# Three rotating PSUM banks for the exponentials, one bank for the product with V, and a new order around the start of the experts

## The chip, the cores and the metric

The kernel runs on one core of a Trainium2 chip. The metric is device time in microseconds (us), from the start to the end of one execution; less is better. The engines named below are TensorE (PE in the rows, its weight loads PEld), VectorE (DVE), ScalarE (ACT), GpSimd (POOL) and SyncE (SP, which issues most DMAs). Each engine runs its own list of instructions in a fixed order and waits on semaphores that the others raise.

## The reference

It is one transformer block in fp32: attention with 16 heads of 16 on 4 sequences of 1024 tokens, then a mixture of 8 experts on all 4096 tokens, 2 experts for each.

```python
# attention, on the normalised x
scores = einsum('bqhd,bkhd->bhqk', Q, K) / sqrt(16)
alpha  = softmax(scores, axis=-1)          # over all keys
alpha  = where(causal, alpha, 0)           # masked only after the softmax
Y      = einsum('bhqk,bkhd->bqhd', alpha, V)
x      = x + layernorm(Y)
# experts, on the normalised x
w, idx = top_k(softmax(x @ router), 2); w = w / sum(w)
for e in range(8):
    out += combine[:, e] * (gelu(x @ w_fc[e]) @ w_proj[e])
x      = x + layernorm(out)
```

The row maximum and the denominator of the softmax run over all 1024 keys, the product with V over the lower triangle only.

## The kernel before, in words

**Prologue** (to about 165 us): Q, K and V of all tokens are computed and the parts of Q and K go through DRAM.

**Attention** works on 16 groups of 4 heads. A group takes 32 *units* (k = 0 to 31 of `body(p, u)`), and the stages of three successive groups overlap: while group p has its scores computed, groups p-1 and p-2 have their exponentials and their product with V. One unit holds:

- the **score pair** (L1261): two 512-column matmuls into banks 0 and 1 or 2 and 3, which DVE reduces to row maxima (`negmax`, L1701) in one instruction of 1024 columns. The pair of unit k waits until the reduction of unit k-2 is done (`s_max`);
- two **chunks** (L1074, or L1067 for the upper corner that only feeds the denominator): one 512-column matmul each, which ACT exponentiates out of PSUM (L921, L916). They take banks 4 and 5 in turn (`ebank`), so a chunk waits for the exponential of the chunk two before it (`s_expB`). In the last group, from its third chunk on, four banks rotate (`LAST_RING`);
- in 12 of the 32 units a **burst** of the product with V (L1104), after four exponentials and, on the diagonal, POOL's mask (L765). Burst b belongs to one half of the queries: halves 1 and 0 accumulate in banks 7 and 6. In the numbering of this text bursts lie in units 13, 16, 18, 21, 24, 26, 29, 0 (half 1) and 2, 5, 8, 10 (half 0);
- in units 1, 9, 17 and 25 the **transposed maxima** (L1274), through banks 6 and 7, copied by ACT (L905);
- after the last burst of a half: DVE copies the bank out (*copy-out*, L1712, `at_poc`, units 1 and 11), PE transposes the copy back into the same bank (*turn*, L1248, `at_turn`, units 3 and 13), DVE normalises from it (*norm*, L1725 and L1730, `at_norm`, units 5 and 15).

In a unit of before, PE runs turn, burst, first chunk, score pair, maxima, second chunk. From p = 6 on, DVE also does the two layer norms of finished groups in units 7 to 26 (`STEADY`).

**Tail**: bodies p = 16 and 17 have no score pair. Units 0 to 47 counted from p = 16 carry the router (`turn_x`, `logits`, `turn_back`, `choose`, `count`, `place`), the table of the first ten expert tiles (`totals_early`, `list_early`, `take_early`), the first gathers, the last layer norms (`four_*`), and the first product of tile 0 (`AT_FIRST`, L1206). The orders come from the tables of `at_*` numbers. In one unit DVE runs its tail steps ahead of copy-out and norm.

**Experts**: 71 tiles of 128 tokens. For each, PE transposes the gathered rows (L1193, `transpose_x`), DVE copies them (`copy_x`, L1653 and L1657), PE runs the first product (L1206) and, after ACT's gelu (L976), the second (L1220); DVE scales (`copy_y`, L1665), POOL scatters. Tiles 0 to 8 are written out by hand, interleaved with the router's last two groups and with the table of the remaining 61 tiles (`list_late`, L1181; `hot`, L1810 and L1815; `indices`).

## Time and profile before

| | |
|---|---|
| median of 3 runs | 1549.6 us (1548.51 to 1550.6) |
| the profiled execution, its own time | 1549.0 us |
| its span, first to last instruction | 1547.1 us |
| PE busy | 1420.5 us, 92% |
| DVE busy | 925.6 us, 60% |
| ACT busy | 805.0 us, 52% |
| POOL busy | 610.7 us, 39% |
| mean granted TensorE clock | 0.979 of 2.4 GHz |

A matmul's duration in the trace is longer than the time it keeps the array: matmuls overlap, so the distance between starts tells what one costs. Busy shares are averages over the stages. The chain of waits follows the work that ended last backwards; its pieces touch one another, and in a run of matmuls their lengths are those distances.

### The profile page before, as it was taken

The page shows a single profiled execution, that of the slowest core. Times are in us where ns is not written, and L with a number is a line of the kernel's source. Part 1 is how long each engine was busy: PE and PEld are TensorE (multiplying, and loading weights), DVE is VectorE, ACT ScalarE, POOL GpSimd, SP SyncE. Part 2 cuts the span into 40 slices and gives each one's busy share as a digit, 9 for nine tenths or more (in the row PEclk, how much of TensorE's full clock was granted, in tenths as well). Part 3 has the DMA queues.
Part 4 walks back from the last instruction along what each step waited for, and adds up shares of the span by engine and source line. Part 5 has one row for each costly group of instructions (what it writes and reads, how often), then busy time and mean ns, then how long its engine had stood idle before and what let it go on. Part 6 is the DMA issues. An engine that isn't in the chain of part 4 may idle for free.

```text
span 1547.1 us, 28642 instructions
## 1 busy us (share of the span) xinstructions
PE 1420.5 (92%) x9774; PEld 822.8 (53%) x9775; DVE 925.6 (60%) x1740; ACT 805.0 (52%) x1717; POOL 610.7 (39%) x729
## 2 busy tenths in 40 slices
PE   6788999999999999999999997989999999999990
PEld 3444233333333233323332333789999999999990
DVE  4587778777888988898888977761111111111115
ACT  5454777777777777777777787221111111111114
POOL 2234434443454445444444442323333333333335
PEclk9999999999999999999999999999999999999995
DMA  3665632112210222022204141656666666666646
GB/s 126 150 159 136 232 42 42 19 24 42 42 31 12 42 42 36 6 42 42 42 1 96 55 137 61 187 136 174 193 174 177 192 173 176 194 173 177 193 113 221
DMA packets 100405, 166.85 MB, mean 108 GB/s; under 512 B 12400, under 2 KB 67568, under 8 KB 100304
## 3 DMA queue, kind: packets, MB, share of 16 engines
q1 hardware_dynamic: 86192, 146.08, 35.2%
q0 software_dynamic: 13632, 18.69, 7.5%
q10 hardware_dynamic: 480, 0.79, 0.3%
q8 instruction: 56, 0.92, 0.3%
q14 instruction: 45, 0.37, 0.1%
HBM read 130.76 MB, written 34.77 MB: 107 GB/s over the span
## 4 chain that ended last, share of the span: by engine, by line
PE 69%; DVE 17%; issue 6%; ACT 5%; POOL 2%; DMA 2%; ACTq 0%; POOLq 0%; DVEq 0%
PE ps L1206 16%; PE ps L1220 16%; PE ps L1104 11%; DVE negmax L1701 10%; PE ps L1074 9%; PE ps L1261 8%; ACT wfc L921 2%; PE ps L1043 2%; PE ps L1067 2%; POOL wfc L833 1%; DVE x L1519 1%; PE ps L1248 1%; PE ps L1193 1%; DVE mv L1508 1%; ACT yx L848 1%
## 5 line engine op out<-in xcount | busy, mean ns | idle before, releaser
L1701 DVE TENSOR_REDUCE negmax<-ps 128x1 f32<-128x1024 f32 x512 | 606.8, 1216 | 133.9 <-PE ps L1261 132.4
L921 ACT ACTIVATE wfc<-ps 128x512 f32<-128x512 f32 x768 | 436.0, 595 | 166.2 <-PE ps L1074 160.4
L976 ACT ACTIVATE wfc<-ps 128x512 f32<-128x512 f32 x142 | 84.8, 597 | 426.3 <-PE ps L1206 399.6
L1206 PE MATMUL ps<-yx,wfc 128*128 128x128 f32 x2272 | 268.1, 276 | 5.3 <-issue 5.3
L1206 PEld LDWEIGHTS ps<-yx,wfc 128*128 128x128 f32 x2272 | 266.2, 193 | 9.5 <-issue 6.3
L1220 PE MATMUL ps<-arena,wfc 128*128 x1136 | 258.7, 381 | 0.3 <-issue 0.3
L765 POOL TENSOR_TENSOR wfc<-wfc,causal 128x512 f32<-128x512 f32 x128 | 162.5, 1270 | 243.2 <-issue 111.3
L821 POOL DMA_INDIRECT expert_out<-wfc,rt x71 | 112.7, 1587 | 299.6 <-DVE wfc L1665 289.2
L1220 PEld LDWEIGHTS ps<-arena,wfc 128*128 128x128 f32 x1136 | 211.4, 191 | 26.9 <-issue 0.8
L1261 PE MATMUL ps<-arena 96*128 96x512 bf16 x704 | 211.6, 382 | 8.6 <-DMA arena<-qk_parts 5.3
L1074 PE MATMUL ps<-arena 120*128 120x512 bf16 x528 | 202.3, 390 | 12.0 <-ACT wfc L921 0.4
L1104 PE MATMUL ps<-wfc 128*16 128x128 f32 (+4 forms) x2304 | 161.2, 381 | 0.5 <-POOL wfc L765 0.5
L1665 DVE TENSOR_SCALAR wfc<-ps,rt 128x256 f32<-128x256 f32 x71 | 34.3, 483 | 205.0 <-PE ps L1220 205.0
L916 ACT ACTIVATE ps<-ps 128x512 f32<-128x512 f32 x256 | 149.5, 584 | 10.6 <-PE ps L1067 1.0
L1074 PEld LDWEIGHTS ps<-arena 120*128 120x128 bf16 x528 | 50.1, 96 | 183.5 <-ACT wfc L921 117.1
L1653 DVE SCALAR_TENSOR_TENSOR rt<-yx,rt 128x1 f32 (+1 forms) x71 | 15.5, 218 | 201.4 <-PE ps L1193 201.4
L1261 PEld LDWEIGHTS ps<-arena 96*128 96x128 bf16 x704 | 67.8, 99 | 62.6 <-issue 12.0
L1104 PEld LDWEIGHTS ps<-wfc 128*17 128x17 f32 (+1 forms) x2304 | 60.7, 97 | 75.6 <-issue 47.0
L1074 PE MATMUL ps<-wfc 120*128 120x512 bf16 x240 | 93.0, 388 | 6.5 <-ACT wfc L921 0.8
L1261 PE MATMUL ps<-wfc 96*128 96x512 bf16 x320 | 95.6, 379 | 0.3
L1104 PE MATMUL ps<-wfc,vone 128*17 128x128 f32 (+3 forms) x1024 | 94.6, 441 | 1.0
L744 POOL TENSOR_TENSOR arena<-mT,dmask 24x1024 bf16<-24x1024 bf16 x44 | 83.3, 1894 | 14.8 <-ACT mT L905 11.8
(208 smaller groups left out, 1259.7 us busy)
## 6 DMA issues: line engine op xcount, KB each, us to landing
wfc<-in_L_ffn_w_fc SPq DMA_DIRECT2D x71, 1024.0 KB
arena<-qk_parts SPq DMA_DIRECT2D x126, 128.0 KB, 5.4
...
```

The lines of the kernel that those rows point to most:

```text
L744: pool.tensor_tensor(qs[(u - back) % NSL][MROW:MROW + MR, hl, :] .rearrange("p (i q) -> p i q", i=QT), mT[MROW:MROW + MR, :].unsqueeze(1). ...
L765: pool.tensor_tensor(md_sb[b % NET], et_sb[b % NET][:, :, q:q + P], causal[:, :].unsqueeze(1).to_broadcast([P, GH, P]), ALU.mult).then_inc ...
L821: pool.indirect_dma_start(out=ys_d, in_=yslot[t % 2], in_offset=None, out_offset=bass.IndirectOffsetOnAxis(ap=tok[:, t:t + 1], axis=0), co ...
L916: nc.scalar.activation(bk(ebank(c, g)), bk(ebank(c, g)), ACT.Exp, accum_out=den_u[:, (u - back) % NSL, hl, i:i + 1]).then_inc(s_expB, 1)
L921: nc.scalar.activation(et_sb[b % NET][:, hl, :], bk(ebank(c, g)), ACT.Exp).then_inc(s_expB, 1)
L976: nc.scalar.activation(hidT[s][:, 4 * hf:4 * hf + 4, :], bk(1 + hf).rearrange("p (c t) -> p c t", c=4), ACT.Gelu).then_inc(s_ge, 1)
L1074: nc.tensor.matmul(bk(ebank(c, g)), ks[v][0:MROW + MR, hl, i * P:(i + 1) * P], qs[v][0:MROW + MR, hl, hf * 512:(hf + 1) * 512], start=True ...
L1104: ins = nc.tensor.matmul(out[32 * hl:32 * hl + rows, q0:q1], lhs, rhs, start=(i == 0 and piece == 0 and n == 0), stop=False, skip_group_ch ...
L1206: ins = nc.tensor.matmul(bk(1 + hf)[:, c * P:(c + 1) * P], w1[s][:, kc * FF + (4 * hf + c) * P:kc * FF + (4 * hf + c + 1) * P], xsT[:, kc, :],
L1220: ins = nc.tensor.matmul(bk(5 + s)[:, 0:D], hidT[s][:, c, :], arena[:, ds(off + c * D, D)], start=(c == 0), stop=(c == FC - 1))
L1261: ins = nc.tensor.matmul(bk(2 * (k % 2) + hf), qs[u][0:SROWS, hl, i * P:(i + 1) * P], ks[u][0:SROWS, hl, hf * 512:(hf + 1) * 512], start=T ...
L1701: nc.vector.tensor_reduce(negmax[:, hl % 2, i:i + 1], ps[:, 2 * (k % 2):2 * (k % 2) + 2, :], AX.XY, ALU.max, negate=True).then_inc(s_max, 1)
```

## The change

Three things move; no arithmetic is added or removed.

1. **The ring.** Banks 4, 5 and 6 rotate over one list, `RING`, that has in PE's order every turn, chunk and (but for group 0) transposed maxima. Entry n waits until entry n-3 has been read: by ACT's exponential if that was a chunk, by ACT's copy if maxima, by DVE's norm if a turn (`ring_free`). Both halves of the product with V use bank 7; the first burst of a half waits for the copy-out of the half before (`s_poc`) and no longer for a norm two bursts back. `LAST_RING` goes.
2. **Order in a unit.** PE runs turn, score pair, burst, first chunk, maxima, second chunk. The norm moves two units earlier, into the unit of its turn.
3. **Ahead of and in the first experts.** New numbers in the tail tables, tile 0 transposed into bank 2, `copy_x(5)` and `copy_x(7)` earlier on DVE, other places for `list_late` on PE, `gather(2)` ahead of a root on POOL.

```diff
-        at_norm = [x + 2 for x in at_turn]
+        at_norm = list(at_turn)
...
-        LAST_RING = (4, 5, 1, 2)
...
-        at_bn_x, at_var_x, at_root_x, at_scale = (4, 42), (5, 44), (5, 44), (7, 46)
+        at_bn_x, at_var_x, at_root_x, at_scale = (4, 44), (5, 45), (5, 45), (7, 46)
...
-        at_place = [x + 11 for x in at_first]
-        AT_TOTALS, AT_LIST, AT_TAKE, AT_INDEX, AT_ROWS, AT_TURN0, AT_COPY0, AT_FIRST = 25, 28, 29, 31, 36, 39, 40, (43, 44)
+        at_place = [x + 11 + 2 * (i == IN_TAIL - 1) for i, x in enumerate(at_first)]
+        AT_TOTALS, AT_LIST, AT_TAKE, AT_INDEX, AT_ROWS, AT_TURN0, AT_COPY0, AT_FIRST = 25, 29, 29, 31, 34, 39, 40, (43, 44)
...
+        def ring_entries():
+
+            out = []
+            for x in range(PRO, (NGR + 2) * U):
+                p, k = divmod(x, U)
+                out += [("turn", p - back, j) for j, back in due(at_turn, k) if live(p, back)]
+                chunks = [("chunk", p - back, c) for c, back in due(at_chunk, k) if live(p, back)]
+                out += chunks[:1]
+                out += [("maxima", p - back, hl) for hl, back in due(at_m, k) if live(p, back)]
+                out += chunks[1:]
+            return out
...
+            def ring_free(kind, g, x):
+                n = SLOT[kind, g, x] - NRING
+                if n < 0:
+                    return
+                last, g, x = RING[n]
+                if last == "chunk":
+                    pe.wait_ge(s_expB, NCH * g + x + 1)
+                elif last == "turn":
+                    pe.wait_ge(s_norm, 2 * g + x + 1)
+                else:
+                    pe.wait_ge(s_mtc, GH * g + x + 1)
...
-                    wait_pos(pe, s_expB, NCH * g + c - 1)
+                ring_free("chunk", g, c)
...
-                    et, out = et_sb[b % NET], bk(6 + hf)
+                    et, out = et_sb[b % NET], bk(7)
...
-                        wait_pos(pe, s_norm, 2 * (g - 1) + (j + 1))
-                        pe.wait_ge(s_mtc, min(GH * g + M_BEFORE_PV[j], NH) if isinstance(g, int) else
-                                   GH * g + M_BEFORE_PV[j])
+                        wait_pos(pe, s_poc, 2 * g + j)
...
-                if isinstance(t, int) and t == 0 and hf == 0:
-                    pe.wait_ge(s_expB, NCH * NGR)
...
             first_product(4, 0)
             transpose_x(5, 1)
             second_product(4, 0)
-            first_half(5, 1, 0)
+            first_product(5, 1)
             list_late(0)
-            first_half(5, 1, 1)
             list_late(1)
-            list_late(2)
             transpose_x(6, 0)
             off = expert(5)
             second_half(5, 1, off, 0)
+            list_late(2)
             list_late(3)
+            second_half(5, 1, off, 1)
             list_late(4)
-            second_half(5, 1, off, 1)
             list_late(5)
+            first_product(6, 0)
+            transpose_x(7, 1)
             list_late(6)
-            first_half(6, 0, 0)
             list_late(7)
-            first_half(6, 0, 1)
-            transpose_x(7, 1)
             first_product(7, 1)
...
             for i in (6, 7):
                 gates(i)
+            copy_x(5, 1)
...
             for q in range(2):
                 hot(q)
-            copy_x(5, 1)
             copy_y(4, 0)
...
-            for q in range(4, NPR // PCE):
+            for q in range(4, 6):
                 hot(q)
             copy_y(5, 1)
+            for q in range(6, NPR // PCE):
+                hot(q)
+            copy_x(7, 1)
...
-            copy_x(7, 1)
             copy_x(8, 0)
```

The first place is PE in a middle group, from the end of unit 1 to the turn of unit 3. Before (L1074 and L1067 are chunks, L1261 score pairs, L1104 the burst, L1248 the turn):

```order
L1074 MATMUL ps<-arena 128x512 [waits s_expB]
L1104 MATMUL ps<-wfc,vone 17x128 [waits s_expB,s_mtc,s_norm]
L1104 MATMUL ps<-wfc,vone 17x128 x3
L1104 MATMUL ps<-wfc 17x384 x4
L1104 MATMUL ps<-wfc 16x128 [waits s_mask]
L1104 MATMUL ps<-wfc 16x128 x3
L1074 MATMUL ps<-arena 128x512 [waits s_expB]
L1261 MATMUL ps<-arena 128x512 [waits s_max]
L1261 MATMUL ps<-arena 128x512
L1067 MATMUL ps<-arena 128x512 [waits s_expB]
L1248 MATMUL ps<-ident,wfc 128x128 [waits s_poc]
L1248 MATMUL ps<-ident,wfc 128x128 x3
```

The change, from the end of unit 1 to the second chunk of unit 2 (L1094 and L1087 are chunks, L1277 score pairs, L1122 the burst):

```order
L1094 MATMUL ps<-arena 128x512 [waits s_expB]
L1277 MATMUL ps<-arena 128x512 [waits s_max]
L1277 MATMUL ps<-arena 128x512
L1122 MATMUL ps<-wfc,vone 17x128 [waits s_expB,s_poc]
L1122 MATMUL ps<-wfc,vone 17x128 x3
L1122 MATMUL ps<-wfc 17x384 x4
L1122 MATMUL ps<-wfc 16x128 [waits s_mask]
L1122 MATMUL ps<-wfc 16x128 x3
L1094 MATMUL ps<-arena 128x512 [waits s_expB]
L1087 MATMUL ps<-arena 128x512 [waits s_mtc]
```

and, right behind it, units 3 and 4 with the turn (L1267):

```order
L1267 MATMUL ps<-ident,wfc 128x128 [waits s_expB,s_poc]
L1267 MATMUL ps<-ident,wfc 128x128 x3
L1277 MATMUL ps<-arena 128x512 [waits s_max]
L1277 MATMUL ps<-arena 128x512
L1094 MATMUL ps<-arena 128x512 [waits s_expB] x2
L1277 MATMUL ps<-arena 128x512 [waits s_max]
L1277 MATMUL ps<-arena 128x512
L1094 MATMUL ps<-arena 128x512 [waits s_norm]
L1087 MATMUL ps<-arena 128x512 [waits s_expB]
```

The score pair stands ahead of the burst, the burst of unit 2 waits for a copy-out, and the first chunk of unit 4 waits for a norm.

The second place is DVE just before the experts (counted units 41 to 44). Before (L1519 and L1500 are a layer norm's add and statistics, L1450 to L1490 `place(5)`, L1712 the last copy-out; twelve rows of `place(5)` lie between the two pieces):

```order
L1519 SCALAR_TENSOR_TENSOR x1<-yx,rstd,x1 128x256 [waits s_rsy]
L1519 SCALAR_TENSOR_TENSOR x1<-yx,rstd,x1 128x256 x3
L1523 TENSOR_TENSOR shift<-mv,rstd 128x4
L1500 BN_STATS stats<-x1 128x6 [waits s_add]
L1500 BN_STATS stats<-x1 128x6 x3
L1450 TENSOR_TENSOR rt<-rt,ps 128x32 [waits s_rank]
```

```order
L1486 TENSOR_SCALAR gsum<-gtmp 128x4 [waits s_ex2]
L1488 RECIPROCAL gate<-gsum 128x4 [waits s_gate]
L1490 SCALAR_TENSOR_TENSOR gate<-gtmp,gate 128x4 [waits s_gate]
L1712 COPY wfc<-ps 128x512 [waits s_T4,s_pv]
L1512 MEMSET pause 128x1 [waits s_bnx]
```

The change (L1535 and L1516 are the add and the statistics, L1728 the copy-out, L1466 the start of `place(5)`):

```order
L1535 SCALAR_TENSOR_TENSOR x1<-yx,rstd,x1 128x256 [waits s_rsy]
L1535 SCALAR_TENSOR_TENSOR x1<-yx,rstd,x1 128x256 x3
L1539 TENSOR_TENSOR shift<-mv,rstd 128x4
L1728 COPY wfc<-ps 128x512 [waits s_T4,s_pv]
L1516 BN_STATS stats<-x1 128x6 [waits s_add]
L1516 BN_STATS stats<-x1 128x6 x3
L1466 TENSOR_TENSOR rt<-rt,ps 128x32 [waits s_rank]
```

The last copy-out stands ahead of the statistics and of `place(5)`.

## Rows read from the trace of the kernel before

**Rows 1.** Busy us (count) of PE, PEld, DVE, ACT, POOL; clock, DMA share, GB/s

```profile
270.00:900.00 630.00, 603.87 (x4315) 199.44 (x4317) 545.98 (x672) 478.32 (x1044) 279.71 (x379) 1.00 0.22 35
```

**Rows 2.** Waits, 270 to 900 us: engine, line, releaser; total us, times, longest

```profile
PEld ps L1074 <- ACT wfc L921: 141.2, 298, 0.9
DVE negmax L1701 <- PE ps L1261: 81.8, 97, 1.4
```

**Rows 3.** Chain of waits in one group: start us, us, what

```profile
345.40 0.44 PE ps L1248 x4
345.84 0.22 PE ps L1074
346.06 0.43 PE ps L1261 x2
...
360.74 0.65 PE ps L1248 x4
...
377.37 1.21 PE ps L1104 x24
...
389.80 1.20 PE ps L1104 x16
```

**Rows 4.** Timeline: start us, us, engine line op, shapes [idle before <-releaser]

```profile
336.27 0.39 PE L1074 MATMUL ps<-arena 120*128 120x512 bf16 x1
...
336.70 1.74 ACT L921 ACTIVATE wfc<-ps 128x512 f32<-128x512 f32 x3 [0.84 <-PE ps L1074]
...
337.13 3.49 DVE L1701 TENSOR_REDUCE negmax<-ps 128x1 f32<-128x1024 f32 x3 [0.95 <-PE ps L1261]
```

**Rows 5.** Timeline of DVE: the last copy-outs of four groups

```profile
309.76 0.68 DVE L1712 COPY wfc<-ps 128x512 f32<-128x512 f32 x1
...
360.00 0.68 DVE L1712 COPY wfc<-ps 128x512 f32<-128x512 f32 x1
...
563.60 0.68 DVE L1712 COPY wfc<-ps 128x512 f32<-128x512 f32 x1
...
614.56 0.67 DVE L1712 COPY wfc<-ps 128x512 f32<-128x512 f32 x1
```

**Rows 6.** Timeline of DVE: a reduction and the norm behind it

```profile
603.88 1.22 DVE L1701 TENSOR_REDUCE negmax<-ps 128x1 f32<-128x1024 f32 x1 [0.91 <-PE ps L1261]
...
605.30 0.42 DVE L1730 TENSOR_TENSOR yx<-ps,rden 128x256 f32<-128x256 f32 x1
```

**Rows 7.** Timeline of DVE just before the experts

```profile
972.41 1.40 DVE L1500 BATCH_NORM_STATS2 stats<-x 128x6 f32<-128x256 f32 x4
...
977.25 0.69 DVE L1712 COPY wfc<-ps 128x512 f32<-128x512 f32 x1
...
979.63 1.38 DVE L1526 TENSOR_SCALAR yx<-x,mv,rstd 128x256 f32<-128x256 f32 x4 [1.19 <-POOL rstd L717]
```

**Rows 8.** Timeline of PE into the experts

```profile
978.00 0.66 PE L1248 MATMUL ps<-ident,wfc 128*128 128x128 f32 x4 [2.46 <-DVE wfc L1712]
...
979.21 5.23 PE L1220 MATMUL ps<-arena,wfc 128*128 x16 [0.34 <-issue]
...
989.83 3.72 PE L1220 MATMUL ps<-arena,wfc 128*128 x16
```

**Rows 9.** Timeline of DVE and PE around the products of tiles 5 to 7

```profile
1016.04 0.16 DVE L1787 SCALAR_TENSOR_TENSOR tots<-tots,ntile 128x8 f32<-128x8 f32 x1
...
1021.37 0.42 DVE L1657 COPY yx<-ps 128x256 f32<-128x256 f32 x1
...
1021.89 3.76 PE L1206 MATMUL ps<-yx,wfc 128*128 128x128 f32 x16 [4.18 <-issue]
...
1040.27 3.81 PE L1206 MATMUL ps<-yx,wfc 128*128 128x128 f32 x32 [1.08 <-issue]
```

**Rows 10.** Busy time in two stretches of rows 8 and 9, columns as above

```profile
979.30:982.00 2.70, 2.70 (x7) 2.16 (x8) 2.30 (x9) 0.00 (x0) 0.30 (x1) 0.50 0.85 213
1020.00:1025.00 5.00, 3.11 (x14) 3.14 (x15) 2.13 (x6) 0.00 (x0) 2.58 (x2) 0.50 0.58 225
```

More of the change, by code:

```diff
@@ L467, in x_bank, with tx_bank @@
             return 0 if i < IN_TAIL or kc == 0 else 4
+        def tx_bank(t):
+            return 2 if isinstance(t, int) and t == 0 else 7
         def at_tail(x, p, k):
@@ L515, in load_side, with ring_bank @@
                    .then_inc(s_ld[u], 16)
+        def ring_entries():
[8 more added lines that the diff above has]
+            return out
+        RING = ring_entries()
+        NRING = 3
+        SLOT = {x: n for n, x in enumerate(RING)}
+        R0 = (2 - SLOT["turn", NGR - 1, 1]) % NRING
+        def ring_bank(kind, g, x):
+            return 4 + (SLOT[kind, g, x] + R0) % NRING
         def turn_bank(hl, g):
-            return 7 if isinstance(g, int) and g == 0 else 6 + HALVES[M_HALF[hl]]
+            return 7 if g == 0 else ring_bank("maxima", g, hl)
+        assert PRO > U + max(at_m) - U and ring_bank("turn", NGR - 1, 1) == 6
         @block.sync
@@ L811, in _ @@
             groups(pool, body)
+            gather(2)
             root_y(NPAIR + 2, TPC)
-            gather(2)
             root_x(NPAIR + 2, TPC)
@@ L910, in body @@
                         g = p - back
+                        bank = bk(ring_bank("chunk", g, c))
                         act.wait_ge(s_ST, NCH * g + c + 1)
@@ L915, in body @@
                                 wait_pos(act, s_dt, g - 2)
-                            nc.scalar.activation(bk(ebank(c, g)), bk(ebank(c, g)), ACT.Exp,
+                            nc.scalar.activation(bank, bank, ACT.Exp,
                                                  accum_out=den_u[:, (u - back) % NSL, hl, i:i + 1]).then_inc(s_expB, 1)
@@ L920, in body @@
                         wait_pos(act, s_pv, NBU * g + b - NET + 1)
-                        nc.scalar.activation(et_sb[b % NET][:, hl, :], bk(ebank(c, g)), ACT.Exp).then_inc(s_expB, 1)
+                        nc.scalar.activation(et_sb[b % NET][:, hl, :], bank, ACT.Exp).then_inc(s_expB, 1)
             root_c(0, 0)
@@ L1073, in chunk @@
                     pe.wait_ge(s_ex, GH * g + hl + 1)
-                nc.tensor.matmul(bk(ebank(c, g)), ks[v][0:MROW + MR, hl, i * P:(i + 1) * P],
+                nc.tensor.matmul(bk(ring_bank("chunk", g, c)), ks[v][0:MROW + MR, hl, i * P:(i + 1) * P],
                                  qs[v][0:MROW + MR, hl, hf * 512:(hf + 1) * 512],
@@ L1187, in transpose_x @@
             def transpose_x(t, s):
[L1188 to L1189 removed]
+                if isinstance(t, int) and t == 1:
+                    pe.wait_ge(s_poc, 2 * NGR)
                 pe.wait_ge(s_xs[s], 16 * (t // 2 + 1) if isinstance(t, int) else t * 8 + 8 * (2 - s))
@@ L1246, in body @@
                         pe.wait_ge(s_poc, 2 * (p - back) + (j + 1))
+                        ring_free("turn", p - back, j)
                         for t in range(HQ):
-                            ins = nc.tensor.transpose(bk(6 + hf)[:, t * P:(t + 1) * P],
+                            ins = nc.tensor.transpose(bk(ring_bank("turn", p - back, j))[:, t * P:(t + 1) * P],
                                                       po_sb[:, (HQ * hf + t) * P:(HQ * hf + t + 1) * P], ident[:, :])
                         ins.then_inc(s_T4, 1)
-                    pieces(p, u, k)
-                    todo = due(at_chunk, k)
-                    chunk(p, u, *todo[0])
                     if live(p, 0):
@@ L1263, in body @@
                         ins.then_inc(s_S, 1)
+                    pieces(p, u, k)
+                    todo = due(at_chunk, k)
+                    chunk(p, u, *todo[0])
                     for hl, back in due(at_m, k):
@@ L1267, in body @@
                         h = GH * (p - back) + hl
-                        if isinstance(p, int) and h == GH:
-                            pe.wait_ge(s_poz, 1)
                         pe.wait_ge(s_sp, 4 * h + 4)
                         turned[0] += 1
-                        past = p - M_AFTER_NORM[hl]
-                        wait_pos(pe, s_norm, 2 * past + (M_HALF[hl] + 1) if not isinstance(p, int) or past >= 0 else 0)
+                        if p - back:
+                            ring_free("maxima", p - back, hl)
                         nc.tensor.matmul(bk(turn_bank(hl, p - back))[MROW:MROW + MR, 0:P],
```

37 lines of the change are left out of this document (11 added, 26 removed).

## The prediction

> **What bounds the kernel now.** I read the slices of the page first: attention takes PE at nine tenths from about 165 to 900 us, the experts take PE whole from about 1060 to 1500, and what lies between is ragged. The change leaves the loop over the expert tiles alone, so an earlier start there passes to the end one for one. Then the busy table of the middle of attention [rows 1]: PE 96%, but with overlapping durations, DVE 87%, ACT 76%, granted clock 1.00. No engine is full, so the limit is a pattern of waits. The list of waits says which [rows 2]: PE's weight load of a chunk waits for an exponential 298 times, 141.2 us, and DVE waits 81.8 us for score pairs. The chain [rows 3] gives prices as distances: turn 0.44, chunk 0.22, score pair 0.43, burst with a diagonal 1.21. One off the diagonal streams 512 instead of 640 columns, 0.97. The timeline [rows 4] gives ACT 1.74 / 3 = 0.58 for each exponential, starting 0.43 after its chunk starts; DVE (3.49 - 1.22) / 2 = 1.14 for each reduction. A release reaches PE in 0.06 (the copy-out of [rows 5] ends at 360.68, the turn starts at 360.74 [rows 3]).
>
> The period of a group is 50.24 us without layer norms and 50.96 with them, from the last copy-outs [rows 5]. PE's own work in a group is 32 units of 0.87 = 27.8, 8 + 4 bursts of 1.30 and 1.07 (0.09 added around each, an estimate) = 14.7, two turns 0.9, four maxima 1.0 (estimate, 0.25 each): 44.4. Some 5.8 are waits. DVE's own work is 32 x 1.14 + 2 x 0.61 + two norms of about 0.7 [rows 6] = 39 without layer norms.
>
> **The ring, walked.** With those prices I walked PE, ACT and DVE from unit to unit: a chunk starts when PE is free and the exponential two (before) or three (after) entries back is over. As a test, from the burst of unit 24 to that of unit 0 the walk of before gives 12.5; the chain has 389.80 - 377.37 = 12.43 [rows 3]. For the change it gives 12.0. So a third bank wins 0.5 in 8 units, not all of the 1.3 lost there: with a burst and a score pair between chunks ACT still starts late, and then three banks fill. The maxima now take an entry, and hold the second chunk 0.3 each time. Over the 27 units from 5 to the next 0 this is -1.5.
>
> **The turns.** (a) Turn of unit 13: its copy-out waits for a reduction plus 0.61, before and after; but DVE gets its score pairs earlier, being ahead of the burst: walk -0.6. (b) New: the burst of unit 2 waits for the copy-out of unit 1. The score pair of unit 1 comes 0.43 + 1.30 + 0.44 after that of unit 0, then reduction 1.14 and copy-out 0.68: PE stands 0.5 (ends 0 and 1.1; part of it would otherwise go to the maxima's entry). (c) New: the first chunk of unit 4 waits for the norm of unit 3. From that unit's score pair 0.60 + 1.14 + 0.70 + 0.06 = 2.5 (the norm runs from 605.02, where the reduction of 603.88 gives way, to 605.72 [rows 6]), of which PE fills 0.43 + 0.44 + 0.43 = 1.3: +1.1 (ends 0.6 and 1.8). (d) The same in unit 14 is mostly covered by the burst of unit 13: +0.3. Units 0 to 5 come to +1.45 against before, (c) included. Group without layer norms: -1.5 - 0.6 + 0.3 + 1.45 = about -0.4. Queued behind (b) and (c) on PE are ACT's chunks and DVE's next score pair; in those units neither is the bound, both catch up.
>
> With layer norms DVE carries some 5.5 us more in units 7 to 26 (44 to 45 against 39), and there the pair ahead of the burst keeps it fed. The walk gives 50.5 against 50.96: -0.5. Some 5 groups at -0.4 and 10 at -0.5: **-7.0 us**. Even a DVE bound in those 20 units and PE in the other 12 would give a group of 47.
>
> By the Trainium skill, "Perfetto Trace Analysis", Matmuls, independent matmul groups should rotate through different PSUM banks, so that the evacuation of one overlaps the next. The product with V stops doing so, the chunks do it more. By the skill's sentence on the product alone the sum would get (b) and (c) without the ring's gain, which is the slower rival below.
>
> **The tail.** Bodies 16 and 17 lose the fourth bank of the last group, and (b) and (c) come once more: **+1.0** (ends 0 and 3). From DVE's statistics and `place(5)` to the copy-out lie 972.41 to 977.25 [rows 7], while PE is done with the first product of tile 0 at 978.00 - 2.46 = 975.54 [rows 8]. With the copy-out first, the turn starts when PE is free. But in unit 35 the norm now stands ahead of `place(4)` and waits for its turn, which puts DVE 1.2 later. Turn about 976.9 instead of 978.0. The second product of tile 0 took 5.23 against 3.72 for tile 1 [rows 8], at a granted clock of 0.50, the 1.2 GHz level [rows 10], after PE had waited 2.46; without that wait I take 3.7. Then `turn_x(6)` needs the scale that stood at 979.63 to 981.0 [rows 7] and now comes near 982.4 behind `place(5)`, which takes 1.2 back: -1.1 - 1.5 + 1.2, rounded with the rest of the walk to **-1.7** (ends -4 and +2). POOL's root for that scale is two steps later and is in it. The gather of tile 0 two units earlier only meets DVE's `choose(5)`, which is the later: 0.
>
> **Copies of tiles 5 and 7.** PE stands 4.18 before the first product of tile 5 and goes on at 1021.89 [rows 9]. The releaser is `copy_x(5)`, which ends at 1021.37 + 0.42 = 1021.79 and stands on DVE behind the table and two `hot`. In the change it follows the gates, at 1016.04: done near 1016.6, before PE is free at 1021.89 - 4.18 = 1017.71. So 4.18 go. With them goes the half clock [rows 10]: 16 matmuls took 3.76, and 32 at full clock 3.81, so 1.85. `copy_x(7)` moves ahead of the index arithmetic, and the 1.08 before 1040.27 go. Behind it `list_late` gets its first two pieces some 0.3 late. Weights of tile 7 are asked for once the first product of tile 5 ends, earlier too. Sum **-6.8** (ends -7.5 and -3, if a wait for weights comes instead).
>
> **Sum.** -7.0 + 1.0 - 1.7 - 6.8 = -14.5. Against the profiled execution's 1549.0 (span 1547.1 and 1.9 around it): 1534.5. The median of the runs is 0.6 higher: **1535 us**. A measurement tells about 0.2%, 3.1 us, from no change.
>
> **Rivals.**
> 1. *Slower: the single bank.* The new waits (b) and (c) come in all 15 groups. If ACT's waits do not shrink (a third bank only shifts them to the maxima's and turn's entries) and (b) and (c) are at their upper ends, a group has +1.1 + 1.8 - 0.6 = +2.3, hence +35 and -8.5 at the experts: 1575. It decides from +0.8 us a group on, where the kernel passes 1552. For it: DVE waits for PE in [rows 2], so a late copy-out finds no slack. Against: the walk agrees with [rows 3]. Chance 0.09.
> 2. *The ring does all it could.* PE's waits for exponentials vanish, some 3 us a group more than in my walk: 1549 - 14.5 - 45 = about 1490. Against: the units with a burst need 1.73 us between chunks and ACT has 3 x 0.58 = 1.74 in hand only if all three banks are full. Half of it, 1512, is as near. Chance 0.13.
> 3. *Attention unchanged, experts earlier.* The gains and the new waits cancel: 1549 - 8.5 + 1 = 1541.5. Chance 0.13.
> 4. *The early copies do nothing*, because the weights of tile 5 or 6 land late: 1549 - 8 = 1541. Chance 0.04, and if attention is no gain either, 1548, 0.03.
> 5. *The clock falls in attention.* [Rows 1] has 1.00 with waits of at most 0.9 us [rows 2]; (b) and (c) stay near 1. If one stretch of 2 us at the low level came in each group, as at tile 0, 15 x 1.5 = +22 and the sum of the rest -14.5: 1557. Chance 0.03. The Trainium skill, "TensorE: Matmul & The Clock Gate", in "A second HAM failure mode: psum-queue depth-cycling", describes such swings in a kernel that cycles PSUM banks. Two banks cycle in this trace without any.
>
> **Numbers.** My forecast has 0.55, with its own range of 1526 to 1543. Range over all, 1515 to 1548: it takes in rivals 3 and 4 and half of rival 2, and leaves out rivals 1 and 5 and the full rival 2. Faster by over 0.2%: the forecast, 2, 3 and most of 4: 0.83. Within it 0.06, from the edge of 3 and 4. Slower 0.11, from 1 and 5.
>
> **What would show it.** Right: period of a group 49.6 to 50.0 without and about 50.4 with layer norms; waits of chunks for exponentials down by a third; a wait of bursts for the copy-out of about 0.5, and of chunks for norms of about 1, once a group; no PE wait over 1 us between 1000 and 1045; clock 1.00 in attention. Wrong: waits of 1.5 us and more in units 2 to 4, a group of 51 or over, or the 4 us at tile 5 still there with another releaser.

## The result

The changed kernel takes **1553.88 us** (median of 10 runs, 1552.46 to 1555.35), beside 1549.42 us of the kernel before (10 runs, 1547.85 to 1550.94). The ratio is 1.0029, 95% interval 1.0019 to 1.0039: slower by 4.5 us. The profiled execution took 1552.65 us, with a span of 1550.7 at a mean clock of 0.981 (before: 1547.1, 0.979). The forecast was 1535.

### The profile page after: what moved, and what is told of

Read it like the earlier page. It is cut to its first block, busy times and chain, and to the rows that moved or that the text cites. A ratio compares the mean times of both kernels' runs of the same rounds, so it can differ in the third digit from the quotient of the medians.

```text
span 1550.7 us, 28662 instructions
## 1 busy us (share of the span) xinstructions
PE 1393.8 (90%) x9774; PEld 822.1 (53%) x9775; DVE 944.7 (61%) x1740; ACT 771.5 (50%) x1717; POOL 611.5 (39%) x729
## 4 chain that ended last, share of the span: by engine, by line
PE 66%; DVE 21%; issue 5%; ACT 3%; POOL 2%; DMA 2%; ACTq 0%; POOLq 0%; DVEq 0%
PE ps L1222 16%; PE ps L1238 15%; DVE negmax L1717 11%; PE ps L1122 10%; PE ps L1277 9%; PE ps L1094 7%; PE ps L1087 2%; PE ps L1054 2%; DVE x L1535 2%; DVE mv L1524 1%; DVE wfc L1728 1%; POOL wfc L843 1%; ACT ps L927 1%; PE ps L1267 1%; PE ps L1211 1%
## 5 line engine op out<-in xcount | busy, mean ns | idle before, releaser
L932 ACT ACTIVATE wfc<-ps 128x512 f32<-128x512 f32 x768 | 423.0, 598 | 237.1 <-PE ps L1094 233.3
L987 ACT ACTIVATE wfc<-ps 128x512 f32<-128x512 f32 x142 | 84.8, 597 | 423.6 <-PE ps L1222 423.6
L775 POOL TENSOR_TENSOR wfc<-wfc,causal 128x512 f32<-128x512 f32 x128 | 162.1, 1267 | 297.2 <-issue 153.4
L1277 PE MATMUL ps<-arena 96*128 96x512 bf16 x704 | 212.0, 383 | 18.4 <-DVE negmax L1717 10.6
L1094 PE MATMUL ps<-arena 120*128 120x512 bf16 x528 | 185.7, 388 | 24.4 <-DVE yx L1746 13.7
L1122 PE MATMUL ps<-wfc 128*16 128x128 f32 (+4 forms) x2304 | 161.3, 382 | 0.1
L927 ACT ACTIVATE ps<-ps 128x512 f32<-128x512 f32 x256 | 153.8, 601 | 0.0
L1094 PEld LDWEIGHTS ps<-arena 120*128 120x128 bf16 x528 | 47.3, 97 | 153.2 <-ACT wfc L932 49.6
L1277 PEld LDWEIGHTS ps<-arena 96*128 96x128 bf16 x704 | 63.9, 99 | 93.2 <-DVE negmax L1717 26.1
L1122 PEld LDWEIGHTS ps<-wfc 128*17 128x17 f32 (+1 forms) x2304 | 60.4, 98 | 87.5 <-issue 63.1
L1122 PE MATMUL ps<-wfc,vone 128*17 128x128 f32 (+3 forms) x1024 | 95.5, 445 | 7.3 <-DVE wfc L1728 7.3
L1277 PE MATMUL ps<-wfc 96*128 96x512 bf16 x320 | 95.7, 380 | 4.5 <-DVE negmax L1717 4.2
L1094 PE MATMUL ps<-wfc 120*128 120x512 bf16 x240 | 84.0, 384 | 14.0 <-DVE yx L1746 8.7
```

The source lines that it names most:

```text
L775: pool.tensor_tensor(md_sb[b % NET], et_sb[b % NET][:, :, q:q + P], causal[:, :].unsqueeze(1).to_broadcast([P, GH, P]), ALU.mult).then_inc ...
L927: nc.scalar.activation(bank, bank, ACT.Exp, accum_out=den_u[:, (u - back) % NSL, hl, i:i + 1]).then_inc(s_expB, 1)
L932: nc.scalar.activation(et_sb[b % NET][:, hl, :], bank, ACT.Exp).then_inc(s_expB, 1)
L987: nc.scalar.activation(hidT[s][:, 4 * hf:4 * hf + 4, :], bk(1 + hf).rearrange("p (c t) -> p c t", c=4), ACT.Gelu).then_inc(s_ge, 1)
L1094: nc.tensor.matmul(bk(ring_bank("chunk", g, c)), ks[v][0:MROW + MR, hl, i * P:(i + 1) * P], qs[v][0:MROW + MR, hl, hf * 512:(hf + 1) * 512 ...
L1122: ins = nc.tensor.matmul(out[32 * hl:32 * hl + rows, q0:q1], lhs, rhs, start=(i == 0 and piece == 0 and n == 0), stop=False, skip_group_ch ...
```

## The profile after

The busy table of the changed kernel for the middle of attention, to be held against [rows 1]: us in the stretch, then busy us and count of PE, PEld, DVE, ACT and POOL, the granted clock, the DMA share and GB/s.

```profile
270.00:900.00 630.00, 571.36 (x4232) 195.67 (x4230) 555.32 (x664) 441.40 (x1022) 274.20 (x374) 1.00 0.23 35
```

The clock stayed at 1.00. DVE is busy 9.3 us more than before although it executes 8 instructions fewer in the stretch. That is the first sign: some of its instructions take longer, it does not run more of them.

The list of waits of the changed kernel, same stretch, answers to [rows 2]: engine and line, the releaser, total us, times, longest. Lines have moved: the chunk L1074 is L1094, the score pair L1261 is L1277, the exponential L921 is L932, the norm L1730 is L1746, the copy-out L1712 is L1728.

```profile
ACT wfc L932 <- PE ps L1094: 184.7, 188, 2.1
...
DVE negmax L1717 <- PE ps L1277: 72.8, 111, 1.6
...
PEld ps L1094 <- ACT wfc L932: 53.2, 136, 0.9
...
PEld ps L1094 <- DVE yx L1746: 29.1, 24, 1.4
...
PE ps L1094 <- DVE yx L1746: 17.3, 24, 0.9
...
PE ps L1122 <- DVE wfc L1728: 5.4, 12, 0.5
```

The ring did its work: PE's waits of chunks for exponentials fall from 141.2 us [rows 2] to 53.2. ACT waits longer for chunks instead: 184.7 us, against 122.5 in the kernel before. The two new waits are there at the size forecast: the burst stands 5.4 / 12 = 0.45 for the copy-out, and the chunk 17.3 / 24 = 0.7 for the norm.

Where the time went is read from the last copy-out of each group, as in [rows 5]. The timeline of DVE in the changed kernel: start us, us, engine, line and shapes.

```profile
308.02 0.68 DVE L1728 COPY wfc<-ps 128x512 f32<-128x512 f32 x1
...
357.90 0.68 DVE L1728 COPY wfc<-ps 128x512 f32<-128x512 f32 x1
...
408.46 0.67 DVE L1728 COPY wfc<-ps 128x512 f32<-128x512 f32 x1
...
512.96 0.67 DVE L1728 COPY wfc<-ps 128x512 f32<-128x512 f32 x1
...
565.20 0.68 DVE L1728 COPY wfc<-ps 128x512 f32<-128x512 f32 x1
...
912.26 0.69 DVE L1728 COPY wfc<-ps 128x512 f32<-128x512 f32 x1
```

A group without layer norms takes 49.88 us (before: 50.24), a group with them 52.25 (before: 50.97 on the mean). Here is the same account for the whole kernel. Its marks are copy-outs: of before at 209.29, 410.71 and 903.16, of the change at 208.26, 408.46 and 912.26 (the third is the first copy-out of the tail, in unit 1 of p = 16):

| stretch | before | after | difference | forecast |
|---|---|---|---|---|
| three groups without layer norms and one in whose last units they begin | 201.42 | 200.20 | -1.2 | -1.6 |
| 9.7 groups with them | 492.45 | 503.80 | **+11.35** | about -5 |
| from there to the end | 643.94 | 638.44 | -5.5 | -7.5 |

The three add up to +4.6; the medians differ by 4.5. (The first of these marks lies between 206.7 and 211.4 us in the kernels of this study, also in those that differ only behind it, so I count from it on.) One row of the table, the groups with layer norms, holds 16 of the 19 us that the forecast missed.

**What lengthened DVE's instructions.** Mean durations in the list of groups, 400 to 900 us. First the kernel before, then the changed one (line, engine, operation, shapes and count, busy us and mean ns, idle time before).

```profile
L1519 DVE SCALAR_TENSOR_TENSOR x<-yx,rstd,x 128x256 f32<-128x256 f32 x20 | 15.3, 767 | 0.0
...
L1508 DVE TENSOR_SCALAR mv<-mv 128x2 f32<-128x2 f32 x10 | 12.1, 1211 | 0.3
...
L1516 DVE TENSOR_SCALAR mv<-mv 128x2 f32<-128x2 f32 x10 | 1.7, 169 | 0.3
```

```profile
L1535 DVE SCALAR_TENSOR_TENSOR x<-yx,rstd,x 128x256 f32<-128x256 f32 x20 | 24.1, 1206 | 0.0
...
L1524 DVE TENSOR_SCALAR mv<-mv 128x2 f32<-128x2 f32 x10 | 18.6, 1858 | 0.3
...
L1532 DVE TENSOR_SCALAR mv<-mv 128x2 f32<-128x2 f32 x10 | 1.7, 170 | 0.3
```

L1524, the last instruction of `var_y`, works on two numbers per partition and takes 1.86 us. L1532, the same form on the same shape in `var_x`, takes 0.17. The timelines of DVE and POOL show what differs. The changed kernel, `var_y` in unit 9 and the second `add` in unit 17:

```profile
522.12 1.89 POOL L754 TENSOR_TENSOR wfc<-mT,dmask 24x1024 bf16<-24x1024 bf16 x1 [1.33 <-ACT mT L915]
...
561.11 1.89 POOL L754 TENSOR_TENSOR arena<-mT,dmask 24x1024 bf16<-24x1024 bf16 x1
```

```profile
522.36 1.94 DVE L1535 SCALAR_TENSOR_TENSOR x<-yx,rstd,x 128x256 f32<-128x256 f32 x1
...
561.17 1.86 DVE L1524 TENSOR_SCALAR mv<-mv 128x2 f32<-128x2 f32 x1
```

And the kernel before in the same units:

```profile
572.54 1.89 POOL L744 TENSOR_TENSOR arena<-mT,dmask 24x1024 bf16<-24x1024 bf16 x1 [0.73 <-ACT mT L905]
...
610.47 1.89 POOL L744 TENSOR_TENSOR arena<-mT,dmask 24x1024 bf16<-24x1024 bf16 x1
```

```profile
573.65 1.06 DVE L1519 SCALAR_TENSOR_TENSOR x<-yx,rstd,x 128x256 f32<-128x256 f32 x1
...
611.19 1.19 DVE L1508 TENSOR_SCALAR mv<-mv 128x2 f32<-128x2 f32 x1
```

In all four pairs the end of the DVE instruction follows that of the GpSimd product beside it: `var_y` ends with the product and the add 0.3 us behind it (561.17 + 1.86 = 563.03 and 561.11 + 1.89 = 563.00; 611.19 + 1.19 = 612.38 and 610.47 + 1.89 = 612.36). In the kernel before `var_y` came 0.72 us into that product, now 0.06: nearly all of it is waited out. The add came 1.11 into it and now comes 0.24 into it. I call the part over the bare duration "held". Bare are 0.17 for `var_y`, 0.475 for an add, 0.40 for a scale. A group of the kernel before has 1.04 + 2 x 0.29 + 2 x 0.19 = 2.0 us held, one of the changed kernel 1.69 + 2 x 0.73 + 2 x 0.20 = 3.5.

The Trainium skill, "SBUF — State Buffer", Who interferes with whom, says that GpSimd and VectorE share a pair of ports as an exclusive lock: a `tensor_scalar` in a two-port mode, or an instruction with two inputs in SBUF, waits in full for a GpSimd instruction that started first (and, for the second form, reads SBUF), and `tensor_reduce` does not. The rows agree: 1.69 us held for the first form and 1.47 for the second (1.94 - 0.475), while reductions beside the same product, as in e3 below, keep their 1.2 us. Which mode `var_y` runs in, the trace does not show.

**Theory A**: the change moves `var_y` and the second `add` under GpSimd's product, DVE loses some 1.5 us more a group, and as DVE is nearly full there, the group gets longer. **Rival B**: the loss is the ring's own, from chunks behind the norm in units 4 and 14 and from DVE waiting for pairs; the held instructions sit in slack.

## Experiments

### VectorE's steps moved away from GpSimd's product

`e1_after_vary8` and `e2_after_add15` each move one of the steps of the changed kernel (e1 takes the statistics that `var_y` needs, `bn_y`, along), `e3_after_both` both and a scale; `e4_before_both` has the three moves in the kernel before.

```diff
 # e1: var_y earlier
-STEADY = {7: ("bn_y", 0), 8: ("bn_y", 1), 9: ("var_y", 0), 13: ("add", 0), 17: ("add", 1),
+STEADY = {6: ("bn_y", 0), 7: ("bn_y", 1), 8: ("var_y", 0), 13: ("add", 0), 17: ("add", 1),
 # e2: add earlier
-STEADY = {7: ("bn_y", 0), 8: ("bn_y", 1), 9: ("var_y", 0), 13: ("add", 0), 17: ("add", 1),
+STEADY = {7: ("bn_y", 0), 8: ("bn_y", 1), 9: ("var_y", 0), 13: ("add", 0), 15: ("add", 1),
 # e3 (in the changed kernel) and e4 (in the kernel before)
-STEADY = {7: ("bn_y", 0), 8: ("bn_y", 1), 9: ("var_y", 0), 13: ("add", 0), 17: ("add", 1),
-          18: ("bn_x", 0), 19: ("bn_x", 1), 20: ("var_x", 0), 24: ("scale", 0), 26: ("scale", 1)}
+STEADY = {6: ("bn_y", 0), 7: ("bn_y", 1), 8: ("var_y", 0), 13: ("add", 0), 15: ("add", 1),
+          18: ("bn_x", 0), 19: ("bn_x", 1), 20: ("var_x", 0), 24: ("scale", 0), 25: ("scale", 1)}
```

> The changed kernel with bn_y and var_y one unit earlier each (6, 7, 8 in place of 7, 8, 9), so that the 128x2 tensor_scalar of var_y is issued before GpSimd's product for the maxima (L754, 1.89 us, 561.11 in the trace of the change) and not beside it. Theory A (VectorE's tensor_scalar stands still until that GpSimd instruction has ended: 1.86 us at 561.17, against .17 for the same form at 528.63): the mean of L1524 falls from 1.86 to about .2, the group with layer norms from 52.25 to about 50.9, and the kernel to 1538 to 1545. Rival B (the loss of 1.3 a group comes from the ring: the chunk of unit 14 behind the norm, maxima behind PE): L1524 may get shorter, the idle time of DVE takes it up, and the time stays at 1554 within 2.

> The changed kernel with the second add of a group at unit 15 in place of 17, ahead of GpSimd's product of unit 18 (522.12, 1.89 us; the add beside it took 1.94 where the first took .47). Theory A: mean of the adds L1535 falls from 1.21 to about .5, 1.3 to 1.5 us a group less on DVE, and the kernel is at 1541 to 1548. Rival B: stays at 1554 within 2, or gets slower, since the add now stands between the norm of unit 13 and the maxima that PE waits for.

> The changed kernel with both steps moved (6, 7, 8 and 15) and the second scale at unit 25 in place of 26 (.81 beside GpSimd's product of unit 26, .40 without it). Theory A: 1.69 + 1.47 + .40 us a group go from DVE, ten groups, of which the idle time of DVE (5.2 us a group) takes up some: 1524 to 1535, and the group near 49.9 to 50.2. Rival B: within 2 us of 1554, with the group at 52.

> The same three moves in the kernel before. There the blocked times were 1.02 (var_y), .59 (add) and .37 (scale) a group. Theory A: 10 to 20 us less, 1530 to 1540, and the change is then worth what the moved-free comparison gives: e3 under e4 by 3 to 12 us (my walk of the ring gave -.5 a group, and the experts -6.8). Rival B: the kernel before stays at 1549 and e3 above it.

Measured beside 1549.72 us of the kernel before (19 runs):

| kernel | us | ratio, 95% interval | group with layer norms |
|---|---|---|---|
| e1 | 1546.76 | 0.998 (0.9971 to 0.9989) | 51.57 |
| e2 | 1542.98 | 0.9961 (0.9947 to 0.9974) | 51.13 |
| e3 | 1537.55 | 0.9919 (0.9906 to 0.9933) | 50.45 |
| e4 | 1546.20 | 0.998 (0.997 to 0.999) | 50.66 |

Rival B falls: a few steps moved by one or two units in DVE's list, with the ring untouched, take 16 us from the changed kernel. The group without layer norms stays at 49.88 in all three. e2 came where Theory A put it; e1 and e3 came 2 to 3 us short of it, and e4 won 3.5 us, not 10 to 20. The kernel before has little to gain from these moves, so the loss belongs to the change; e3 is 8.7 us under e4, where 3 to 12 was expected. What was still held in e1 and e3 is in their rows. The timelines of POOL and of DVE in e3:

```profile
555.80 1.26 POOL L775 TENSOR_TENSOR wfc<-wfc,causal 128x512 f32<-128x512 f32 x1 [0.27 <-ACT wfc L932]
...
557.14 1.89 POOL L754 TENSOR_TENSOR arena<-mT,dmask 24x1024 bf16<-24x1024 bf16 x1
```

```profile
555.85 0.15 DVE L1522 BATCH_NORM_AGGREGATE mv<-stats 128x2 f32<-128x6 f32 x1
...
556.03 1.06 DVE L1524 TENSOR_SCALAR mv<-mv 128x2 f32<-128x2 f32 x1
...
557.00 3.64 DVE L1717 TENSOR_REDUCE negmax<-ps 128x1 f32<-128x1024 f32 x3
```

`var_y` had moved from one product of GpSimd to another, the mask (L775), and ended with it (557.09 and 557.06). The aggregate beside the same mask was not held, and three reductions under the 1.89-us product took 3.64 together.

### All held time away, and what is left of the change

`f1_after_vary12` puts `var_y` where GpSimd is nearly idle. `f2_before_vary12` has the same edit in the kernel before; there the scales were still held, and `m2_before_free` moves those too.

```diff
 # f1, f2
+STEADY = {7: ("bn_y", 0), 8: ("bn_y", 1), 12: ("var_y", 0), 14: ("add", 0), 15: ("add", 1),
+          18: ("bn_x", 0), 19: ("bn_x", 1), 20: ("var_x", 0), 24: ("scale", 0), 25: ("scale", 1)}
+ROOT_Y, ROOT_X = 13, 21
 # m2 against f2
-          18: ("bn_x", 0), 19: ("bn_x", 1), 20: ("var_x", 0), 24: ("scale", 0), 25: ("scale", 1)}
+          18: ("bn_x", 0), 19: ("bn_x", 1), 20: ("var_x", 0), 23: ("scale", 0), 26: ("scale", 1)}
```

> The changed kernel with var_y at unit 12 (its root at 13), the adds at 14 and 15 and the second scale at 25: no GpSimd instruction over .7 us runs there. In e1 and e3 the moved tensor_scalar still took 1.06 us, and ended with the product with the mask of unit 9 (L775, 555.80, 1.26 us): Theory A says any of GpSimd's products holds it, so here it takes .17, the group comes to 49.9 to 50.2 (e3: 50.45), and the kernel to 1531 to 1535. Against A: L1524 stays near 1 us wherever it is put, because it reads what bn_aggr has just written, and the time stays with e3 (1537.6).

> The kernel before with the same moves as f1 (var_y at unit 12 with its root at 13, adds at 14 and 15, second scale at 25), so that neither kernel has a step of the layer norms beside a product on GpSimd. Theory A: L1508 takes .17 here; the group goes from 50.66 (e4) to about 50.5, the kernel to 1544 to 1546, and f1 stands under it by 11 to 12 us: what the change is worth without the blocking. If the blocked time is what the change loses, its gain is then near my forecast for it (-7.0 in the attention and -6.8 in the experts, with +1.3 between). Against A: f2 is as far under before as f1 is under the change (20 us, at 1529), and the moves help any order alike.

> The kernel before with var_y at unit 12, its root at 13, the adds at 14 and 15 and the scales at 23 and 26, where GpSimd runs no product over .7 us. Held time 0 in a group with layer norms. Theory A with the slopes so far (50.97, 50.66, 50.39 at 2.0, 1.3 and .7 us held): 50.2 to 50.35, and the kernel 1541 to 1543. Then the change is worth nothing (0 within .1) in such a group where nothing is held, and my walk's -.5 was wrong there by as much. If it stays at 50.39 or above (the scales were not on any path): the change is worth -.1 there.

f1: **1533.50 us** (4 runs), ratio 0.9893 (0.9877 to 0.991). f2: 1543.05 (5 runs), 0.9959 (0.9945 to 0.9973). m2: 1543.04 (4 runs), 0.9954 (0.9937 to 0.997). So the moves do not help any order alike: beside the kernel before measured with each, f1 wins 16.3 us and f2 6.4, though the change by itself had lost 4.5. f1 is 9.5 us under f2, a little less than the 11 to 12 expected. The rows of f1 by form, 400 to 900 us, have nothing held:

```profile
L1542 DVE TENSOR_SCALAR yx<-x,mv,rstd 128x256 f32<-128x256 f32 x20 | 8.0, 402 | 0.0
L1524 DVE TENSOR_SCALAR mv<-mv 128x2 f32<-128x2 f32 x10 | 1.7, 169 | 0.3
```

Held time (worked out as above from each kernel's means) against the period of a group with layer norms:

| changed kernel and its variants | held us | period | before and its variants | held us | period |
|---|---|---|---|---|---|
| change | 3.5 | 52.25 | before | 2.0 | 50.97 |
| e1 | 2.8 | 51.57 | e4 | 1.3 | 50.66 |
| e2 | 2.1 | 51.13 | f2 | 0.7 | 50.39 |
| e3 | 0.9 | 50.45 | m2 | 0 | 50.39 |
| f1 | 0 | 50.28 | | | |

From e3 up to the change, the changed kernel pays 0.7 us for each held (52.25 - 50.45 = 1.8 for 2.6 us). The kernel before pays 0.45 for each above 0.7 (50.97 - 50.39 = 0.58 for 1.3 us). The last 0.9 and 0.7 us cost 0.17 and nothing. With nothing held the change is worth 50.28 - 50.39 = -0.1 in such a group, and with about 2 us held in both (e2 and before) it costs 0.2. In m2 the slopes did not go on as Theory A had them; it is the other of its two outcomes, in which the scales were on no path.

### GpSimd made to wait, VectorE left alone

So far it was DVE that moved. `m1_after_root9` moves one number of GpSimd's.

```diff
-ROOT_Y, ROOT_X = 10, 21
+ROOT_Y, ROOT_X = 9, 21
```

> The changed kernel with one number changed: GpSimd's root of var_y at unit 9 in place of 10. It waits for var_y, so the product for the maxima of unit 10 (1.89 us), which is behind it on GpSimd, can only start when var_y has ended; no step of VectorE is moved. Theory A: L1524 falls from 1.86 to .17 to .5 us, the group from 52.25 to 51.0 to 51.2, the kernel to 1540 to 1545; the add of unit 17 stays at 1.94. Against A (var_y takes 1.86 for a reason of its own, or GpSimd's later product holds up the chunks that wait for it): L1524 or the group unchanged, 1553 or more.

Measured: 1546.45 us (10 runs), ratio 0.9976 (0.9966 to 0.9986), 7.4 us under the change; group 51.57. Timelines of DVE and POOL:

```profile
559.32 0.17 DVE L1524 TENSOR_SCALAR mv<-mv 128x2 f32<-128x2 f32 x1
559.40 1.22 DVE L1717 TENSOR_REDUCE negmax<-ps 128x1 f32<-128x1024 f32 x1
561.53 1.22 DVE L1717 TENSOR_REDUCE negmax<-ps 128x1 f32<-128x1024 f32 x1 [0.92 <-PE ps L1277]
```

```profile
559.64 0.69 POOL L722 TENSOR_TENSOR rstd<-mv,mhalf 128x2 f32<-128x2 f32 x1 [0.45 <-DVE mv L1524]
560.41 1.89 POOL L754 TENSOR_TENSOR arena<-mT,dmask 24x1024 bf16<-24x1024 bf16 x1
```

`var_y` is at the same place in DVE's list and takes 0.17. It is GpSimd's product that holds it. The period fell by 0.68, less than the 1.1 to 1.2 expected, though all 1.69 us are gone: the second reduction behind it now waits 0.92 for its score pair, so PE is late next. e1, with 0.9 of `var_y` still held, has the same period of 51.57: the last 0.9 us of that instruction were covered there, and are not why e1 fell short. m1 has 1.9 us held and a period of 51.57, e2 has 2.1 and 51.13, so the slope of the table is no law: which step is held counts too.

### Which part of the change moved VectorE under the product

`h2_before_pair_first` puts the score pair ahead of the burst in the kernel before; `h1_after_pair_last` puts it back behind them in the changed kernel.

```diff
 # h2, in PE's body (h1 is the reverse)
+                    if live(p, 0):
...
+                        ins.then_inc(s_S, 1)
                     pieces(p, u, k)
                     todo = due(at_chunk, k)
                     chunk(p, u, *todo[0])
-                    if live(p, 0):
...
-                        ins.then_inc(s_S, 1)
```

> The kernel before with the score pair ahead of the burst and the chunk in each unit, ring of two banks kept. If the order alone made the gain of the groups and the loss of those with layer norms: period 49.9 and 52.2, so 1558 to 1562 (without the experts' gain). If the ring made them: period near 50.24 and 50.97, 1549 within 3.

> The changed kernel with the score pair behind the burst and the chunk again, all else as changed. If pair first carries the gain of .36 a group without layer norms, the period of 49.88 goes to 50.2 or more and that of 52.25 changes with the place of DVE against GpSimd (51 to 53): 1548 to 1562. If order is indifferent (DVE and PE lie bound by what they wait for, not by who comes first): 1554 within 2.

Both missed what I expected, by far. h2: 1580.25 us (4 runs), ratio 1.0201 (1.0184 to 1.0218), groups 52.0 and 53.19. h1: 1612.07 us (4 runs), ratio 1.0401 (1.0384 to 1.0419), groups 54.2 without layer norms and up to 57.5 with them. Neither half of the change can stand alone. Groups without layer norms, where hardly anything is held: 50.24 before, 52.0 with the pair first, 54.2 with the ring and the early norm, 49.88 with both. In h1 the first chunk of unit 14 waits for the norm of unit 13, which stands behind that unit's reduction on DVE, and the pair of unit 14, DVE's next work, stands behind the chunk. The timeline of PE in h1:

```profile
326.00 0.39 PE L1094 MATMUL ps<-arena 120*128 120x512 bf16 x1 [1.93 <-DVE yx L1746]
```

The change has 0.19 at that place (311.99), because there the pair of unit 14 is issued before the wait. Where the 1.8 us a group go that h2 loses without layer norms, I have not traced: PE, ACT and DVE show waits of the same kinds as in the kernel before, and that stays open.

h2 answers the question, too. The timelines of DVE and POOL:

```profile
575.63 1.86 DVE L1508 TENSOR_SCALAR mv<-mv 128x2 f32<-128x2 f32 x1
```

```profile
575.57 1.89 POOL L744 TENSOR_TENSOR arena<-mT,dmask 24x1024 bf16<-24x1024 bf16 x1
```

Same offset as in the change, 0.06 us, with the old ring and the old norm. The order "score pair first" moves DVE's step 0.66 us forward against the product. A likely reason, read from the code and not tried by itself: the reduction of a unit starts with its pair, which now comes earlier in the unit, while the maxima that start GpSimd's product are still turned at the unit's end. What a held step costs differs, too: with as much held as in the change (3.6 us by the same means), a group with layer norms in h2 is only 53.19 - 52.0 = 1.2 us longer than one without, where the change has 2.4.

### The experts and the tail

`g1_before_experts` has only the experts' part in the kernel before. `k4_f1_old_tail` is f1 with the unit numbers of the tail as before; `k1_f1_add_later` is f1 with one tail step moved.

```diff
 # g1: DVE (PE's order from first_product(5, 1) on as in the change)
                 gates(i)
+            copy_x(5, 1)
...
-            copy_x(5, 1)
             copy_y(4, 0)
...
+            copy_x(7, 1)
             nc.vector.tensor_reduce(tabf[:, 0:NLC], cmp_l[0:1, :, :], AX.X, ALU.add).then_inc(s_hic, 1)
 # k4
-at_bn_x, at_var_x, at_root_x, at_scale = (4, 44), (5, 45), (5, 45), (7, 46)
+at_bn_x, at_var_x, at_root_x, at_scale = (4, 42), (5, 44), (5, 44), (7, 46)
-at_place = [x + 11 + 2 * (i == IN_TAIL - 1) for i, x in enumerate(at_first)]
+at_place = [x + 11 for x in at_first]
-AT_TOTALS, AT_LIST, AT_TAKE, AT_INDEX, AT_ROWS, AT_TURN0, AT_COPY0, AT_FIRST = 25, 29, 29, 31, 34, 39, 40, (43, 44)
+AT_TOTALS, AT_LIST, AT_TAKE, AT_INDEX, AT_ROWS, AT_TURN0, AT_COPY0, AT_FIRST = 25, 28, 29, 31, 36, 39, 40, (43, 44)
 # k1
-at_bn_y, at_var_y, at_root_y, at_add = (0, 38), (1, 39), (1, 39), (3, 41)
+at_bn_y, at_var_y, at_root_y, at_add = (0, 38), (1, 39), (1, 39), (4, 41)
```

> The kernel before with only the experts' part of the change: copies of the rows of tiles 5 and 7 earlier on VectorE, the late list's products later on TensorE. My ledger: -6.8, so 1542.5 to 1544; the waits of 4.18 and 1.08 at L1206 are gone. If the -9.5 that the change won between the turn of tile 0 and tile 8 came from elsewhere (the clock, rows waiting for gathers): 1547 to 1550.

> f1 with the numbers of the units behind the last group as they were before the change (bn_x 42, var_x and root_x 44, place(5) at +11, early list at 28, rows at 36). My prediction gave those numbers +.4 to +1 in all with the start of the tail; g1 and the ledger say +1.3 for all that lies between copy-out and turn. If the numbers are worth something to the new ring: k4 slower than f1 by 1 to 4 us. If they are neutral: 1533.5 within 1.

> f1 with the four adds of the first tail step at unit 4 in place of 3. In f1 they stand ahead of the norm of unit 3 on VectorE, 3.41 us at 895.66 and 1.22 of the shift (1.67 and .16 where GpSimd is idle), and PE waits 2.49 us at 900.89 for that norm. Theory (the norm moved two units earlier now stands behind work that it stood ahead of in time): the wait goes to under .5, the copy-out of unit 11 comes 1.5 to 2.5 us earlier, the kernel 1531 to 1532.5. Rival (the unit 7 to 11 work waits for POOL's root and the scale anyway, 4.35 us of idle at 907.12): same as f1, 1533.5.

g1: 1542.07 us (4 runs), ratio 0.9951 (0.9934 to 0.9967). Its profile from the copy-out at 903.21 to the end takes 637.1 us, before it took 643.9: **-6.8**, the forecast to the tenth (-7.7 by the medians). The timeline of PE in g1 has no wait before the products of tiles 5 and 7, which stood 4.18 and 1.08 in [rows 9]:

```profile
1017.89 3.73 PE L1206 MATMUL ps<-yx,wfc 128*128 128x128 f32 x32
...
1033.33 3.79 PE L1206 MATMUL ps<-yx,wfc 128*128 128x128 f32 x32
```

The change takes 638.4 from its copy-out to the end, so the rest of its tail costs 1.3 against g1. k4: 1536.88 us (4 runs), 0.9916 (0.99 to 0.9933): the new unit numbers are worth 3 us to the new ring (from the first copy-out to the end 1325.8 us, f1 1322.8). k1: 1532.14 us (4 runs), 0.9889 (0.9873 to 0.9906). The wait it aims at is gone. PE in f1, then in k1:

```profile
900.89 0.39 PE L1094 MATMUL ps<-wfc 120*128 120x512 bf16 x1 [2.49 <-DVE yx L1746]
```

```profile
895.93 0.39 PE L1094 MATMUL ps<-wfc 120*128 120x512 bf16 x1 [0.23 <-DVE yx L1746]
```

By the medians k1 and f1 can't be told apart (1.4 us, overlapping intervals, measured beside different runs of the kernel before). In the profiled executions it is 1.9 us from the first copy-out to the end. So k1 is probably the fastest kernel here; that both are 16 to 17 us faster than the kernel before, and some 20 faster than the change, is shown.

## Why the prediction was wrong

- **The walk of the ring, groups without layer norms: right.** Forecast -0.4, measured -0.36 in each. The waits of chunks for exponentials fell by more than the third that was forecast, from 141.2 to 53.2 us, and the group still won no more than that: rival 2 is out. In the group from 308 to 358 us the waits (b), (c) and (d) are 0.45 (341.13), 0.92 (345.76) and 0.19 (311.99), forecast 0.5, 1.1 and 0.3. The clock stayed at 1.00, so rival 5 is out, as is rival 1 in its mechanism: the single bank does not cost more than it was given.
- **The step that failed: "With layer norms DVE carries some 5.5 us more in units 7 to 26 (44 to 45 against 39), and there the pair ahead of the burst keeps it fed. The walk gives 50.5 against 50.96: -0.5."** Measured +1.28 a group. The walk took the 5.5 us as a constant carried over from the kernel before. 2.0 us of them were no work of DVE at all but time held by GpSimd, and that depends on when DVE comes, which is the very thing the change moves. In the change they became 3.5. f1 and m2 size it: with the held time gone the change wins 52.25 - 50.28 = 1.97 a group and the kernel before 50.97 - 50.39 = 0.58; the difference is 1.39 of the 1.78 us between forecast and result. Both kernels also had steps moved to other units for it, so part of the 1.39 may be the place of the steps and not the holding. m1, which leaves DVE's order alone, shows 0.68 of it for `var_y`; the adds and scales were not tried that way. The other 0.39 is the walk itself, which gave -0.5 where -0.1 is left with nothing held. What it overlooked there no run settles. In the stretch this is 16 us of the 19 that the forecast missed.
- **The order of the forecast's gain made the loss.** "The pair ahead of the burst keeps it fed" names the cause of the harm: h2 shows that this order alone brings `var_y` to 0.06 us behind the start of the product.
- **Copies of tiles 5 and 7: right.** -6.8, shown by g1. There the first product of tile 5 takes 3.73 us for 32 matmuls where 16 took 3.76 [rows 9], so the half clock went with the wait, as forecast.
- **Tail start and tile 0: too good by 2.** Forecast +1.0 and -1.7, measured +1.3 in all. From the first copy-out of the tail to the turn ahead of tile 0's second product lie 78.7 us in the change and 74.8 before, and what is behind the turn is 2.4 us shorter than in g1. Of the 3.9, 2.4 lie between the first two copy-outs (16.0 against 13.7): the norm of unit 3 stood behind four adds of 3.41 us and made PE wait 2.5. k1 takes that wait away. In my walk the norm, two units earlier, had only the reduction in front of it on DVE. The other 1.5 I put down to the norm of unit 35, which waits for its turn. I had put DVE 1.2 late for that. The timeline of DVE shows 3.53, and that of PE a wait of 3.64 for DVE's `oh_bf`, which the router's `choose` writes behind it:

```profile
972.18 0.26 DVE L1741 RECIPROCAL rden<-ps 128x16 f32<-128x16 f32 x1 [3.53 <-PE ps L1267]
```

```profile
983.13 0.21 PE L1173 MATMUL ps<-oh_bf,lower 128*128 128x32 bf16 x1 [3.64 <-DVE oh_bf L1455]
...
985.82 5.32 PE L1222 MATMUL ps<-yx,wfc 128*128 128x128 f32 x32
...
991.63 3.62 PE L1238 MATMUL ps<-arena,wfc 128*128 x16
```

The second product of tile 0 did fall from 5.23 to 3.62, as forecast. But the half clock had only moved: the granted clock is 0.50 from 983 to 986 us, behind the wait of 3.64, and the first product takes 5.32, where it took 3.84 at 1.00 in the kernel before. So the term of -1.5 came to nothing. That the wait of 3.64 comes from the norm of unit 35 is read from the chain of waits, and no run takes it away.

- **Rivals.** None was this one. The slower rival looked for its price on PE's new waits; the price was on DVE, beside an engine (POOL, 44% busy) that I had not looked at. The list of groups of before had the mark: a `tensor_scalar` on 128x2 at 1.21 us beside one at 0.17. The forecast's own sign of being wrong, a group of 51 us or over, did come.
